# First expert phase of a macaron block: x loaded first, statistics a tile a step, routing tables between ticks, clears one by one

## What is computed

```python
x = x + 0.5 * ffn(layernorm(x))
x = x + mamba2(layernorm(x))
x = x + 0.5 * ffn(layernorm(x))
```

```python
logits = x @ router_w.T                       # 8 experts
scores, top_idx = jax.lax.top_k(logits, 2)    # raw logits are the weights
h = silu(x @ wg[e]) * (x @ wu[e])             # 512 -> 256
moe = sum of score * (h @ wd[e]) over the two chosen experts
shared = (silu(x @ sg_w + sg_b) * (x @ su_w + su_b)) @ sd_w + sd_b
out = moe + shared
```

## Time and profile before

| | us |
|---|---|
| median of 3 runs | 2311.66 (2310.14 to 2315.39) |
| profiled execution: its time | 2313.75 |
| profiled execution: its span, first to last instruction | 2312.0 |
| PE busy | 2156.3 (93%) |
| DVE busy | 1474.8 (64%) |
| ACT busy | 1432.8 (62%) |
| POOL busy | 1376.3 (60%) |
| first phase ends, last phase begins | 360.7, 1953.6 |

### The profile page before, as it was taken

The page is one execution under the profiler, slowest core; times in us unless marked ns, Lnnn a source line. Parts: engine busy times, 40 slices in busy tenths (PEclk is TensorE's granted clock), DMA queues, the critical chain, the costliest instruction groups (busy, mean ns, idle before and its releaser), DMA issues. The chain is left out here.

```text
span 2312.0 us, 42896 instructions
## 1 busy us (share of the span) xinstructions
PE 2156.3 (93%) x11718; PEld 1744.5 (75%) x11718; DVE 1474.8 (64%) x2947; ACT 1432.8 (62%) x2960; POOL 1376.3 (60%) x1242
## 2 busy tenths in 40 slices
PE   5899996899999999999988999999999997789996
PEld 3687774688888888888767888888888885577775
DVE  6532247577777677777887777777777778732225
ACT  5133323777787778787658787778777774423331
POOL 2886351476666667666517666667666663586622
PEclk8999997899999999999999999999999998899998
DMA  9665361334334333433214434334433431555545
GB/s 345 243 189 175 115 174 42 101 111 108 106 84 119 106 101 99 119 97 93 65 49 127 110 86 126 98 98 105 113 102 88 117 85 35 186 188 164 160 142 164
DMA packets 204904, 285.32 MB, mean 123 GB/s; under 512 B 16288, under 2 KB 148458, under 8 KB 204816
## 3 DMA queue, kind: packets, MB, share of 16 engines
q1 hardware_dynamic: 185936, 219.18, 33.1%
q0 software_dynamic: 18880, 65.02, 9.3%
HBM read 225.43 MB, written 58.72 MB: 123 GB/s over the span
## 5 line engine op out<-in xcount | busy, mean ns | idle before, releaser
L2057 PE MATMUL mamba_p_proj<-mamba_xt_lo,mamba_in_hi 128*128 128x512 f32 x1056 | 456.9, 433 | 1.6 <-DVE mamba_bc L1708 1.1
L1708 DVE SCALAR_TENSOR_TENSOR mamba_xs<-mamba_p_proj,mamba_taps,mamba_xs 128x511 f32<-128x511 f32 (+2 forms) x384 | 285.8, 744 | 258.9 <-ACT mamba_xs L1455 250.0
L2059 PE MATMUL mamba_p_proj<-mamba_xt_hi,mamba_in_lo 128*128 128x512 f32 x1056 | 416.2, 394 | 0.0
L2058 PE MATMUL mamba_p_proj<-mamba_xt_hi,mamba_in_hi 128*128 128x512 f32 x1056 | 414.0, 392 | 0.0
L1328 POOL TENSOR_TENSOR mamba_xend<-mamba_xdt,mamba_to_end_g 128x512 f32<-128x512 f32 x128 | 134.0, 1047 | 340.0 <-DVE mamba_xdt L1768 282.8
L1334 POOL TENSOR_TENSOR mamba_mix<-mamba_mix,mamba_scores 128x512 f32<-128x512 f32 x256 | 326.5, 1297 | 14.2 <-ACT mamba_mix L1521 14.2
L1517 ACT ACTIVATE mamba_mix<-mamba_cum_l,mamba_cum_g 128x128 f32<-128x128 f32 x1024 | 324.7, 388 | 8.7 <-DMA mamba_cum_l<-mamba_cum_rows 3.8
L664 DVE TENSOR_TENSOR ffn_h<-ffn_p_gu,ffn_sil 128x256 f32<-128x256 f32 x110 | 46.8, 426 | 317.9 <-ACT ffn_sil L546 303.9
L546 ACT ACTIVATE ffn_sil<-ffn_p_gu 128x256 f32<-128x256 f32 x110 | 42.3, 385 | 319.4 <-PE ffn_p_gu L913 237.5
L2059 PEld LDWEIGHTS mamba_p_proj<-mamba_xt_hi,mamba_in_lo 128*128 128x128 f32 x1056 | 199.6, 189 | 46.5
L2057 PEld LDWEIGHTS mamba_p_proj<-mamba_xt_lo,mamba_in_hi 128*128 128x128 f32 x1056 | 200.7, 190 | 40.7 <-DVE mamba_bc L1708 2.0
(11 more groups left out here) (344 smaller groups left out, 5095.0 us busy)
## 6 DMA issues: line engine op xcount, KB each, us to landing
mamba_cum_l<-mamba_cum_rows SPq DMA_DIRECT2D x128, 512.0 KB, 5.3
mamba_rise<-mamba_exp_rows SPq DMA_DIRECT2D x256, 128.0 KB, 3.4
ffn_xs<-slots_in SPq DMA_DIRECT2D x78, 256.0 KB, 2.7
slots_out<-ffn_y SPq DMA_DIRECT2D x78, 256.0 KB
mamba_raw_x<-in_t SPq DMA_DIRECT2D x34, 512.0 KB, 5.5
mamba_raw_z<-in_t SPq DMA_DIRECT2D x32, 512.0 KB, 6.4
mamba_raw_out<-out_t SPq DMA_DIRECT2D x32, 512.0 KB, 4.7
slots_out<-ffn_xs SPq DMA_DIRECT2D x1, 9984.0 KB
```

Of the source, the lines that this page charges most:

```text
L1708: dve.scalar_tensor_tensor(dst[:, i:BLK], p_proj[:, ct, 0:BLK - i], tap[:, 0, j:j + 1], dst[:, i:BLK], ALU.mult, ALU.add).then_inc(s_conv, 1)
L2057: pe.matmul(bank, in_hi[:, piece, kk, :], xt_lo[:, kk, c], start=(kk == 0), stop=False)
L2058: pe.matmul(bank, in_hi[:, piece, kk, :], xt_hi[:, kk, c], start=False, stop=False)
L2059: last = pe.matmul(bank, in_lo[:, piece, kk, :], xt_hi[:, kk, c], start=False, stop=(kk == KT - 1))
```

## The change

- SP loads all four blocks of x ahead of the router and the biases.
- POOL issues the shared expert's three weight loads behind its constants, in the first phase; in both phases the loads of weights 2 come behind both scatters.
- DVE makes statistics two blocks ahead, one or two tiles after each low_l (`ahead`), with the block's variance after the third; in the first phase blocks 0 and 1 are done before the steps begin. `roots` moves to the end of a block's last step.
- Each of the eight clears of slots_in waits for the landing of the one before it.
- `turns` is cut in three and `order_pairs` in two, and a tick stands between the pieces; the first piece comes one tick earlier.

```diff
@@ ffn_phase
+        def ahead(t):
+            first, count = ((0, 2), (2, 1), (3, 1), (4, 0))[t % TPB]
+            first += (t // TPB + 2) * TPB
+            return range(first, first + count) if first < T else range(0)
@@ sync
             if hidden is not None:
-                load_x(0)
+                for b in range(NB):
+                    load_x(b)
             sp.dma_start(router[:, :, :], ...
...
             if hidden is not None:
-                for b in range(1, NB):
-                    load_x(b)
                 sp.wait_ge(s_zero, 1)
...
             for e in range(E):
                 row = sp.value_load(free_i[0:1, e:e + 1], ...
+                if e > 0:
+                    sp.wait_ge(s_zeroed, 16 * (e + 2 * (hidden is not None)))
                 sp.dma_start(slots_in[bass.ds(row, P), :], xs[:, 0, :]).then_inc(s_zeroed, 16)
@@ gpsimd
             build_identity(pool, ident[:, :], s_const, 0)
-            load_gate(0)
-            load_up(0)
-            load_out(0)
+            if hidden is None:
+                load_gate(0)
+                load_up(0)
+                load_out(0)
...
+            if hidden is not None:
+                load_gate(0)
+                load_up(0)
+                load_out(0)
             load_gate(1)
             load_up(1)
             load_out(1)
             scatter(0)
+            scatter(1)
             load_gate(2)
             load_up(2)
             load_out(2)
-            scatter(1)
@@ scalar
                 if t + AHEAD < T:
-                    if (t + AHEAD) % TPB == 0 and not known:
-                        roots((t + AHEAD) // TPB)
                     rows(t + AHEAD)
+                if t == 0 and not known:
+                    roots(1)
                 high_l(t)
-                if known and t % TPB == TPB - 1 and t // TPB + known < NB:
-                    roots(t // TPB + known)
+                if t % TPB == TPB - 1 and t // TPB + 2 < NB:
+                    roots(t // TPB + 2)
@@ vector
+            def stat_tile(t):
+                if hidden is not None and t % TPB == 0:
+                    dve.wait_ge(s_x[t // TPB], 16)
+                if t > known * TPB:
+                    dve.wait_ge(s_stat, 2 * (t - known * TPB))
+                dve.bn_stats(stat[:, t % TPB, :], x[:, t, :]).then_inc(s_stat, 1)
+
+            def moments_tile(t):
+                dve.wait_ge(s_stat, 2 * (t - known * TPB) + 1)
+                dve.bn_aggr(moments[:, t, :], stat[:, t % TPB, :]).then_inc(s_stat, 1)
...
             if not known:
                 stats(0)
                 scale(0)
+                stats(1)
             for t in range(T):
-                b = t // TPB + max(known, 1)
-                if known and t % TPB == 0 and known < b <= NB:
-                    scale(b - 1)
-                if t % TPB == 0 and b < NB:
-                    stats(b)
+                if t % TPB == 0 and known <= t // TPB + 1 < NB:
+                    scale(t // TPB + 1)
                 low_l(t)
-                if not known and t % TPB == 0 and b < NB:
-                    scale(b)
+                for u in ahead(t):
+                    stat_tile(u)
+                    moments_tile(u)
+                if t % TPB == TPB - 2 and t + 2 * TPB < T:
+                    variance(t // TPB + 2)
...
             tick(1)
+            turns_first()
             tick(2)
-            turns()
+            turns_second()
             tick(3)
+            turns_third()
+            tick(4)
             order_pairs()
-            for g in range(4, JOBS):
+            tick(5)
+            share_pairs()
+            for g in range(6, JOBS):
                 tick(g)
```

More of the change, by code:

```diff
@@ L619, in stats, with variance @@
                     dve.bn_aggr(moments[:, b * TPB + t, :], stat[:, t, :]).then_inc(s_stat, 1)
-                dve.wait_ge(s_stat, n + 2 * TPB)
+                variance(b)
+            def stat_tile(t):
[7 more added lines that the diff above has]
+                dve.bn_aggr(moments[:, t, :], stat[:, t % TPB, :]).then_inc(s_stat, 1)
+            def variance(b):
+                dve.wait_ge(s_stat, (b - known + 1) * 2 * TPB)
                 s = slice(b * TPB, (b + 1) * TPB)
@@ L753, in places, with turns_first @@
                 dve.tensor_copy(slot[:, :, ts], slot_f[:, :, ts]).then_inc(s_route, 1)
-            def turns():
+            def turns_first():
                 step = link(dve, s_rank, 42)
@@ L764, in turns, with turns_second @@
                 step(dve.tensor_scalar(gap[:, :], count[:, :], -1.0, float(ROOM), ALU.mult, ALU.add))
+            def turns_second():
+                step = link(dve, s_rank, 48)
                 step(dve.tensor_tensor(passed[:, :, :], end[0:1, :].unsqueeze(1).broadcast_to([1, TILES, E]),
@@ L771, in turns, with turns_third @@
                 step(dve.tensor_tensor(wrap[:, 0, :], wrap[:, 0, :], tile_no[:, :], ALU.add))
+            def turns_third():
+                step = link(dve, s_rank, 53)
                 step(dve.tensor_scalar(table[:, 3, :], wrap[:, 0, :], float(P), None, ALU.mult))
@@ L792, in order_pairs, with share_pairs @@
                 step(dve.tensor_tensor(ordered[:, 1, :], slot_f[:, 0, :], slot_f[:, 1, :], ALU.max))
+            def share_pairs():
+                step = link(dve, s_rank, 70)
                 step(dve.tensor_scalar(weight[:, :, :], best[:, :, :], 0.5, None, ALU.mult))
```

## The result

The change made the kernel **slower**: a median of 2354.62 us (2352.55 to 2357.58) against 2312.29 us (2310.14 to 2315.39), ratio 1.0183, 95% interval 1.0165 to 1.0201, which is 42 us. 2298.5 had been predicted, with 2292 to 2309 as the range. Later comparisons ran on four chips. So there are two losses to explain: a small one, found on all three, and a large one that only the first comparison showed.

The account below looks back on a forecast made before the run. PE was taken to bound the expert jobs, so each phase's first transposed tile decides. 6.4 us (first phase) plus 6.8 (last) made 13.2 us, against the median of 2311.66: 2298.5 us, range 2292 to 2309.

Parts of the forecast that it names:

- Part 4: Clears one by one, tables in pieces: most ACT idleness goes, PE reaches columns(9) at 92 to 97 and 2032 to 2036.
- Rival (a): Expert phases: ACT's idleness stays, as the scatter itself may cause it; gain only 3.8 us, to 2307.9; chance 0.2.
- W: First phase: time the first weights' up half lands, for which ACT waits; taken as 24 us, range 21 to 27.
- Part 1: First phase, x first and statistics a tile a step: the scatter starts at 48.9, 4.9 us earlier.
- Part 2: Both phases, expert 2's weights behind the scatter: scatter ends 2.3 us earlier, tile lands in 3.4 us, 0.8 more.
- Part 3: Last phase, statistics a tile a step: slots 1.9 us later, yet tile at 2035.6 against 2042.41, 6.8 us gained.
- rival (b): Both phases: clears bind, 2324 us at 5.0 each; chance 0.06 above 4.2 us per clear, 0.14 between 3.4 and 4.2.

Follow-up runs that it names:

- the front undone: The changed kernel with x's later blocks, the first weight loads and the statistics as in the kernel before: 2291.84 us, ratio 1.0010 to the kernel before.

## Why the prediction was wrong

**The step that failed for the 38 us** is a sentence of Part 4: "I expect most of ACT's unexplained idleness to go", because the DMA peak from 74 to 92 goes. The peak went (share 0.97 to 0.65), and the idleness grew: the waits for "remote" before silu in 60 to 140 us went from 17.3 to 33.9. The prediction's own sign of being wrong, silus "remote" for over 5 us, came true. Rival (a) fits better, that the scatter itself causes the waits, and stopped short of what it could imply: if they come with the scatter, removing the scatter's only break may make them longer. Why they grew stays open. The Trainium skill (Runtime: NRT & Kernel Launch, "Instruction fetch mechanics"), which rival (a) named, says that fetching code is mostly hidden. The profile's queues list the same 48 and 40 packets of instructions for both kernels, so the amount fetched doesn't tell them apart; no row shows what a fetch costs.

Off the first chip, where this plays no part, the forecast gain of 13.2 us became a loss by two terms that were priced too low, W in Part 1 and the landing of the tile in Part 2, and by a gain that was only there to be had on the first chip (Part 3).

**What bounds.** Right everywhere but on the first chip: PE waits for the tile at columns(9) (11.1 us in the kernel before on the second chip, 12.0 in the changed one). On the first chip PE waited only 0.72 us for its tile in the kernel before, so there was hardly room for a gain from an earlier tile alone, and in the changed kernel PE came 9.8 us after it.

**Part 1, 4.9 us expected, 0.2 measured.** The chain was right step by step and one term was mis-sized: W, taken as 24 with 27 as the end of the range, was 28.6. The prediction has xn(7) 1 us behind W (29.59, yes), xn(12) 11.65 behind W (40.32 is 11.7, yes), the scatter 13.2 behind xn(12) (53.55, yes). With the weights at the queue's head the predicted times appear: 24.7, 35.5 and 48.6 for 25.0, 35.65 and 48.9. The gate and up halves, issued at 17.1 and 18.0 behind the router, landed 9.5 and 10.6 us later in a stretch that moves 386 GB/s (first row of the stretches above), where the prediction had given them half the rate.

**Part 2, 2.3 us earlier, tile at 3.4 us.** On the second chip the scatter, from its first DMA to its last, is 2.5 us shorter in the first phase and 2.4 in the last. But the tile lands after 6.2 us in both phases. The prediction took 3.4 from the 2.6 to 4.6, median 2.9, of the kernel before's loads, the first of which had no weights just ahead of it. It had the collision in its text, and undersized it by 2.8 us in each phase.

**Part 3, 1.9 us later in the last phase.** Measured 2.4: first xn to first scatter is 32.4 us before, 34.9 after, and 32.4 with the front undone. But the gain of 6.8 was reckoned from 2042.41. Ahead of that SP had issued the tile's load at 2035.56, 5.6 us after the scatter's last issue ended at 2029.95, where it took 2.5 us on the second chip; the load landed after 4.5 us (2.8 there), and PE took the tile 2.4 us later (at once there). These 7 us were the first chip's, not the order's.

With the measured terms the sum is right off the first chip: first phase 0.2 + 2.5 - 3.3 = -0.6 us, measured -0.7; last phase -2.4 + 2.4 - 3.4 = -3.4, measured -3.4.

**Part 4.** The clears one by one take 3.0 us each where 3.1 was forecast, the last landing by 91.2, and hide behind the scatter; undone, they give less than 1 us, which can't be told from nothing. The Trainium skill (DMA: Bandwidth & Descriptors, "Anatomy of one DMA") gives its 2.0 us of fixed cost for DMAs that GpSimd issues; the estimate of 2.6 us for a clear of 256 KB that the prediction worked out from it agrees with the median landing of 2.6 us on the second chip, though SP issues these. On the first chip they took 4.9, over the 4.2 from which rival (b) decides, but the last of them (103.97) still came before the tables' end (110.39), so it was not they that held the tile.

Tables in pieces were costed at nothing. That holds where product(3) is in time: on the second chip the last third takes 2.0 us from 74.34 on. On the first chip it fell beside POOL's splits; DVE's rows, then POOL's:

```profile
102.46 2.23 DVE L806 TENSOR_SCALAR ffn_wrap<-ffn_turn 1x39 f32<-1x39 f32 x1
...
105.16 2.60 DVE L809 TENSOR_TENSOR ffn_table<-ffn_wrap,ffn_turn 1x39 int32<-1x39 f32 x1
107.79 2.36 DVE L810 CAST ffn_table<-ffn_turn 1x39 int32<-1x39 f32 x1
...
102.27 2.40 POOL L395 TENSOR_TENSOR ffn_in_lo<-ffn_raw_in,ffn_in_hi 128x1024 fp32r<-128x1024 f32 x1
...
105.78 1.92 POOL L393 TENSOR_TENSOR ffn_in_hi<-ffn_raw_in,ffn_one 128x1024 fp32r<-128x1024 f32 x1
107.77 2.34 POOL L395 TENSOR_TENSOR ffn_in_lo<-ffn_raw_in,ffn_in_hi 128x1024 fp32r<-128x1024 f32 x1
```

Steps that take 0.17 to 0.19 us on the second chip take 2.2 to 2.6 here, and each ends within 0.1 us of the end of one of POOL's splits. The Trainium skill (SBUF — State Buffer, "SBUF: two separate sides") says that these two engines share a pair of ports under an exclusive lock, held for a whole instruction, where DVE's operation is in a two-port mode or has two inputs in SBUF. The rows agree: the steps between them that take 0.17 to 0.19 us run where POOL has no split (104.73 to 105.12 in its gap from 104.67 to 105.78). L809 doesn't quite fit: it begins 0.6 us before its split and still ends with it, where by the Trainium skill the one that starts first gets the pair. The last third so took 9.5 us, 101.03 to 110.55, in place of 2.0. It delayed the tile's load, but the tile still lay ready for 9.8 us. What it can have cost is what PE waited for DVE's low_h behind it, 3.1 us at 111.37. That last step is a reading of one profile; no run without the late signals could test it.

## What to carry to other kernels

A transfer that is moved behind another has to be followed to what it then stands in front of: 1.5 MB ahead of a 256 KB load made its landing 6.2 us for 2.8, and ahead of the scatter's end 6.4 for 2.7; let the load that the next stage waits for go first, by a wait if need be (10 us here, 7.0 of them explained). If something will stand ahead of a load, price it by a row in which something does. And a wait whose releaser the profile can't name is a reason to profile the kernel on a second chip before building on it.

## What the runs showed of the hardware

In the first comparison, and on none of the four later chips, while GpSimd issued indirect DMAs, TensorE's semaphore increments came up to 27 us late, its matmuls 0.7 to 2.8 us apart, and SP's register steps took 0.68 us for 0.03; the same programs elsewhere showed none of it. Beside the later chips it cost the kernel before 22 us and the changed kernel 60. The traces show signals that catch up about a pause of the scatter or behind its end (77.14 and 77.69 before, 99.29 and 99.83 after), and others that come late but within a running scatter (89.07 before, 68.20 after). That the missing pause is what lengthened the waits is argued, not shown, and what set the first comparison apart isn't known.
